# A MoE block on one core: skip terms moved from VectorE to ScalarE, and the router as four f32r passes one gate-up pair later

## The reference

```python
x = L0_attn_x
x = x + _L0_attn_ref(_layernorm(x, axis=-1), ...)      # Q (K^T V) scaled, times wo
x = x + _L0_ffn_ref(_layernorm(x, axis=-1), ...)
...
scores = jax.nn.sigmoid(x @ Wr)                        # 8 experts
_, idx = lax.top_k(scores + router_bias, TOP_K)        # two of them
w = jnp.take_along_axis(scores, idx, axis=-1)
w = w / (jnp.sum(w, axis=-1, keepdims=True) + 1e-09)
...
hid = jax.nn.silu(g) * u                               # experts 0 to 3, 256 -> 128 -> 256
mlp_out = jnp.einsum('tei,eih->teh', hid, Wd)
routed = jnp.einsum('te,teh->th', cw[:, :E_MLP], mlp_out)
routed = routed + cw[:, E_MLP:E_MLP + 1] * x
routed = routed + cw[:, E_MLP + 2:E_MLP + 3] * x
routed = routed + cw[:, E_MLP + 3:E_MLP + 4] * jax.nn.relu(x)
...
return routed + SHARED_SCALE * shared                  # shared: causal conv of 4 taps, per feature
```

## Time and profile before

| | us |
|---|---|
| median of 3 runs (lowest, highest) | 961.61 (958.10, 962.31) |
| the profiled execution: time | 958.19 |
| its span, first to last instruction | 956.4 |
| busy: TensorE, VectorE, GpSimd, ScalarE | 893.9, 832.3, 553.2, 544.4 |
| granted TensorE clock, mean share of full speed | 0.98 |

### The profile page before, as it was taken

How to read it: one execution, slowest core, us unless ns; L and a number is a source line. 1 busy time by engine, 2 the same in 40 slices (tenths; PEclk the granted TensorE clock), 3 DMA queues, 4 the chain that set the end, 5 groups by cost and what they waited for, 6 DMA issues and landing times.

```text
span 956.4 us, 16244 instructions
## 1 busy us (share of the span) xinstructions
PE 893.9 (93%) x5402; PEld 768.0 (80%) x5402; DVE 832.3 (87%) x2327; ACT 544.4 (57%) x1076; POOL 553.2 (58%) x491
## 2 busy tenths in 40 slices
PE   4578999999999999999999999999999999888887
PEld 3466888888888888888888888888888888777776
DVE  3677998999899998999999998999989987777885
ACT  3445566556656665666566556656655665444442
POOL 2145556667555566765556666555666764456653
PEclk9968999999999999999999999999999999999999
DMA  5302322223332221333322133332212222222111
GB/s 165 111 22 89 111 94 78 68 95 111 112 111 102 93 82 58 111 111 111 111 89 81 54 110 111 111 111 99 102 45 89 89 89 90 88 68 88 67 45 67
DMA packets 61011, 87.05 MB, mean 91 GB/s; under 512 B 4480, under 2 KB 56832, under 8 KB 56832
## 3 DMA queue, kind: packets, MB, share of 16 engines
q1 hardware_dynamic: 60928, 86.01, 25.9%
HBM read 68.96 MB, written 17.04 MB: 90 GB/s over the span
## 4 chain that ended last, share of the span: by engine, by line
DVE 43%; PE 20%; ACT 13%; POOL 11%; issue 11%; DMA 2%; POOLq 0%; ACTq 0%; SPq 0%; DVEq 0%
ACT x L719 5%; DVE hid L819 5%; ACT x L763 5%; DVE stats L865 4%; DVE acc L857 4%; POOL rstd L1073 4%; POOL enx L1108 3%; DVE acc L1019 3%; DVE idxf L902 3%; PE ps_gu L365 3%; PE ps_sh L464 3%; PE ps_gu L367 2%; PE ps_gu L366 2%; DVE acc L969 2%; PE ps_sh L474 2%
## 5 line engine op out<-in xcount | busy, mean ns | idle before, releaser
L1091 POOL TENSOR_TENSOR gate<-gate,cwb 128x512 f32<-128x512 f32 x128 | 169.3, 1323 | 148.2 <-ACT gate L647 99.8
L365 PE MATMUL ps_gu<-x2T_hi,wgu_hi 128*128 128x512 f32 x512 | 212.8, 416 | 0.9 <-DVE hid L819 0.8
L366 PE MATMUL ps_gu<-x2T_lo,wgu_hi 128*128 128x512 f32 x512 | 203.2, 397 | 0.0
L367 PE MATMUL ps_gu<-x2T_hi,wgu_lo 128*128 128x512 f32 x512 | 203.1, 397 | 0.0
L1108 POOL TENSOR_TENSOR enx<-inv_e,logits 128x32 f32<-128x32 f32 x32 | 178.0, 5561 | 6.7 <-ACT logits L640 6.5
L365 PE MATMUL ps_y<-wd_hi,hid_hi 128*128 128x256 f32 x512 | 156.6, 306 | 8.6 <-POOL hid_lo L1096 7.8
L367 PE MATMUL ps_y<-wd_hi,hid_lo 128*128 128x256 f32 x512 | 145.3, 284 | 0.0
L366 PE MATMUL ps_y<-wd_lo,hid_hi 128*128 128x256 f32 x512 | 145.2, 284 | 0.0
L836 DVE SCALAR_TENSOR_TENSOR conv<-x2T,conv_w,conv 128x512 f32<-128x512 f32 x192 | 143.0, 783 | 0.0
L1070 POOL TENSOR_TENSOR mv<-mv,eps_ln 128x4 f32<-128x4 f32 x64 | 12.8, 200 | 220.7 <-DVE mv L868 175.8
L647 ACT ACTIVATE gate<-ps_gu 128x512 f32<-128x512 f32 x128 | 75.9, 593 | 99.0 <-PE ps_gu L367 99.0
(11 more groups left out here) (100 smaller groups left out, 1834.9 us busy)
## 6 DMA issues: line engine op xcount, KB each, us to landing
cwb<-cw_rows SPq DMA_DIRECT2D x32, 1024.0 KB, 4.7
xa<-in_x SPq DMA_DIRECT2D x32, 512.0 KB, 6.7
acc<-in_x SPq DMA_DIRECT2D x32, 512.0 KB, 5.9
out<-acc SPq DMA_DIRECT2D x64, 256.0 KB, 2.2
cwb<-in_wg SPq DMA_DIRECT2D x4, 128.0 KB, 2.6
cwb<-in_wu SPq DMA_DIRECT2D x4, 128.0 KB, 2.6
cwb<-in_wd SPq DMA_DIRECT2D x1, 512.0 KB, 4.7
cw_rows<-cwT SPq DMA_DIRECT2D x32, 8.0 KB, 1.3
```

The lines of the kernel that those rows point to most:

```text
L365: nc.tensor.matmul(dst, a_hi, b_hi, start=start, stop=False, skip_group_check=True)
L366: nc.tensor.matmul(dst, a_hi, b_lo, start=False, stop=False, skip_group_check=True)
L367: return nc.tensor.matmul(dst, a_lo, b_hi, start=False, stop=stop, skip_group_check=True)
L1091: g.tensor_tensor(gate[:, e % 2], gate[:, e % 2], cwb[:, q, e], ALU.mult).then_inc(gatew_ready, 1)
```

## The change

Router: the weights `wr2` hold the high part of the router's 256 x 8 weights in columns 0 to 7, their low part in columns 8 to 15, and zeros. Four f32r matmuls of 512 columns (x2T high and low, two halves) give the logits of all 512 tokens transposed, ScalarE copies them (`logitsT`), TensorE transposes them back in four (`logits_transpose`), ScalarE copies 64 columns (`parts`), and GpSimd adds the two halves. On TensorE the router now stands behind gate_up 3, and the transposes behind gate_up 4. VectorE's `route` loses the `den` add to GpSimd and finds the chosen experts by `match_replace` instead of `max_index` and comparisons. The terms coef * x2 become acc * (1 + coef * rstd) + coef * shift on ScalarE, with the factors from four small GpSimd instructions (`skip_factors`). The relu add moves from behind hidden 1 to behind `q_low`.

```diff
             def router(st):
-                pe.wait_ge(x2T_ready, st.before("R", HC, HC))
+                if st.before("R") == 0:
+                    pe.wait_ge(wrlo_out, 1)
+                b, q = ps_sh[0], st.slot("R", 2)
                 pe.wait_ge(x2Tlo_ready, st.before("R", HC, 1))
-                b, q = ps_sh[0], st.slot("R", 2)
+                for c in range(HC):
+                    if c == 1:
+                        pe.wait_ge(x2Thi_ready, st.before("R", HC, HC))
+                    nc.tensor.matmul(b[:, :], wr2[:, c], x2T_hi[:, q, c], start=(c == 0), stop=False,
+                                     skip_group_check=True)
+                    if c == 1:
+                        pe.wait_ge(x2Tlo_ready, st.before("R", HC, HC))
+                    last = nc.tensor.matmul(b[:, :], wr2[:, c], x2T_lo[:, q, c], start=False, stop=(c == HC - 1),
+                                            skip_group_check=True)
+                last.then_inc(router_done, 1)
+
+            def logits_transpose(st):
+                pe.wait_ge(logitsT_ready, st.before("R", 1, 1))
                 for t in range(TG):
-                    for c in range(HC):
-                        last = nc.tensor.matmul(b[:, t * NE:(t + 1) * NE],
-                                                x2T[:, q, c, PAD + t * P:PAD + (t + 1) * P], wr_sb[:, c],
-                                                start=(c == 0), stop=(c == HC - 1))
-                last.then_inc(router_done, 1)
+                    last = nc.tensor.transpose(ps_sh[0][:, t * P:(t + 1) * P], logitsT[:, t * P:(t + 1) * P],
+                                               ident[:, :])
+                last.then_inc(parts_done, 1)
...
                 elif st.on("R"):
-                    pe.wait_ge(logits_ready, st.before("R", 1, 1))
+                    pe.wait_ge(parts_ready, st.before("R", 1, 1))
...
@@ -590,16 +616,17 @@
                     gate_up(st, 2)
                 if m_on:
                     chain_et(st)
-                if r_on:
-                    router(st)
+                if c_on:
+                    gate_up(st, 3)
                 if m_on:
                     pe.wait_ge(et_out, st.chains(2, 2))
-                if c_on:
-                    gate_up(st, 3)
-                if m_on:
                     chain_f(st)
+                if r_on:
+                    router(st)
                 if c_on:
                     gate_up(st, 4)
+                if r_on:
+                    logits_transpose(st)
                 if c_on:
                     conv_transpose(st)
...
-                if r_on:
-                    act.wait_ge(router_done, st.before("R", 1, 1))
-
-                    if st.later("R", 1):
-                        act.wait_ge(enx_ready, st.before("R"))
-                    copy(logits[:, :], ps_sh[0][:, 0:TG * NE]).then_inc(logits_ready, 1)
                 if m_on:
                     chain_copy(st, f_done, st.chains(1, 1),
                                [(f1[:, :], ps_gram[:, 0:H]), (f2[0:D, :], ps_gram[0:D, 0:H])], fhi_out)
                 if c_on:
                     hid_high(st, 0)
+                if r_on:
+                    act.wait_ge(router_done, st.before("R", 1, 1))
+                    copy(logitsT[:, :], ps_sh[0][:, :]).then_inc(logitsT_ready, 1)
                 if c_on:
                     silu(st, 2)
+                if r_on:
+                    act.wait_ge(parts_done, st.before("R", 1, 1))
+                    if st.later("R", 1):
+                        act.wait_ge(logits_ready, st.before("R"))
+                    copy(parts[:, :, :], ps_sh[0][:, :].rearrange("p (t n) -> p t n", t=TG)[:, :, 0:2 * NE])\
+                        .then_inc(parts_ready, 1)
+                if c_on:
 
                     q = st.slot("C", 2)
+                    act.wait_ge(skip_ready, st.before("C", 2, 2))
                     for t in range(TG):
-                        act.wait_ge(ident_added, st.before("C", TG, t + 1))
+                        a = acc[:, st.slot("C", 4), t]
+                        nc.scalar.activation(a, a, ACT.Identity, bias=skip_bias[:, q, t:t + 1],
+                                             scale=skip_scale[:, q, t:t + 1]).then_inc(ident_added, 1)
+                    for t in range(TG):
                         nc.scalar.activation(x2[:, q, t], x2[:, q, t], ACT.Relu, scale=cw[:, q, EM + 3, t:t + 1])\
                             .then_inc(relu_ready, 1)
                     hid_high(st, 1)
...
-                dve.wait_ge(enx_ready, st.before("R", 1, 1))
-                done(v.tensor_scalar(den[:, :], enx[:, :], 1.0, None, ALU.add))
-                after()
+                dve.wait_ge(den_ready, st.before("R", 1, 1))
                 done(v.reciprocal(flat(score[:, :, :]), den[:, :]))
                 after()
-                done(v.tensor_tensor(biased[:, :, :], score[:, :, :],
+                done(v.tensor_tensor(biased[:, :, 0:NE], score[:, :, :],
                                      bias8[:, :].unsqueeze(1).broadcast_to([P, TG, NE]), ALU.add))
                 turn(rt, st.before("R", RT, issued[0]))
                 for t in range(TG):
-                    done(v.max(top8[:, t], biased[:, t]))
+                    done(v.max(top8[:, t], biased[:, t, 0:NE]))
+                after()
+                done(v.tensor_copy(two8[:, :, 0:2], top8[:, :, 0:2]))
                 turn(rt, st.before("R", RT, issued[0]))
                 for t in range(TG):
-                    done(v.max_index(idx8[:, t], top8[:, t], biased[:, t]))
+                    done(v.match_replace(marked[:, t], two8[:, t], biased[:, t], TAKEN))
                 after()
-                done(v.tensor_copy(idxf[:, :, :], idx8[:, :, 0:2]))
-                after()
-                for n in range(2):
-                    done(v.tensor_tensor(hot[:, n], iota_f[:, :].unsqueeze(1).broadcast_to([P, TG, NE]),
-                                         idxf[:, :, n:n + 1].broadcast_to([P, TG, NE]), ALU.is_equal))
-                after()
-                done(v.tensor_tensor(chosen[:, :, :], hot[:, 0], hot[:, 1], ALU.add))
-                after()
-                done(v.tensor_tensor(raw[:, :, :], chosen[:, :, :], score[:, :, :], ALU.mult))
+                done(v.scalar_tensor_tensor(raw[:, :, :], marked[:, :, 0:NE], TAKEN, score[:, :, :],
+                                            ALU.is_equal, ALU.mult))
...
-                dve.wait_ge(cw_ready, st.before("R", 1, 1))
-                done(v.tensor_tensor(coef[:, q], cw[:, q, EM], cw[:, q, EM + 2], ALU.add))
...
@@ -1002,21 +1033,11 @@
                     hid_low(st, 0)
                     hidden(st, 1)
 
-                    q = st.slot("C", 2)
-                    dve.wait_ge(rt, st.before("C", RT, RT))
-                    for t in range(TG):
-                        a = acc[:, st.slot("C", 4), t]
-                        v.scalar_tensor_tensor(a, x2[:, q, t], coef[:, q, t:t + 1], a, ALU.mult, ALU.add)\
-                            .then_inc(ident_added, 1)
                 if m_on:
                     dve.wait_ge(fhi_out, st.chains(2, 2))
                     v.tensor_tensor(f2[D:P, :], ps_gram[D:P, 0:H], f1[D:P, :].bitcast(F32), ALU.subtract)\
                         .then_inc(flo_out, 1)
                 if c_on:
-
-                    dve.wait_ge(relu_ready, st.before("C", TG, TG))
-                    k = st.slot("C", 4)
-                    v.tensor_tensor(acc[:, k], acc[:, k], x2[:, st.slot("C", 2)], ALU.add).then_inc(relu_added, 1)
                     hidden(st, 2)
                 if r_on and c_on:
                     route(st)
@@ -1032,6 +1053,12 @@
                     hidden(st, 3)
                 if st.on("Q"):
                     q_low(st)
+                if c_on:
+
+                    dve.wait_ge(ident_added, st.before("C", TG, TG))
+                    dve.wait_ge(relu_ready, st.before("C", TG, TG))
+                    k = st.slot("C", 4)
+                    v.tensor_tensor(acc[:, k], acc[:, k], x2[:, st.slot("C", 2)], ALU.add).then_inc(relu_added, 1)
...
+            def skip_factors(st):
+
+                q = st.slot("R", 2)
+                pool.wait_ge(cw_ready, st.before("R", 1, 1))
+                if st.later("R", 2):
+                    pool.wait_ge(ident_added, st.before("R", TG, -TG))
+                g.tensor_tensor(coef[:, :], cw[:, q, EM], cw[:, q, EM + 2], ALU.add).then_inc(coef_ready, 1)
+                pool.wait_ge(coef_ready, st.before("R", 1, 1))
+                g.tensor_tensor(coef_rstd[:, :], coef[:, :], rstd2[:, q], ALU.mult).then_inc(coefr_ready, 1)
+                g.tensor_tensor(skip_bias[:, q], coef[:, :], shift2[:, q], ALU.mult).then_inc(skip_ready, 1)
+                pool.wait_ge(coefr_ready, st.before("R", 1, 1))
+                g.tensor_tensor(skip_scale[:, q], coef_rstd[:, :], ones4[:, :], ALU.add).then_inc(skip_ready, 1)
+
...
                 if r_on:
+                    pool.wait_ge(parts_ready, st.before("R", 1, 1))
```

(13 more changed lines are left out.)

77 lines of the change are left out of this document (51 added, 26 removed).

## The result

| | median us | lowest, highest | runs |
|---|---|---|---|
| before | 959.92 | 958.10, 962.31 | 4 |
| changed | 1074.72 | 1067.46, 1077.98 | 4 |

The changed kernel takes 1.119 times as long (95% interval 1.1154 to 1.1222). Its profiled execution took 1074.62 us, with a span of 1072.8 and a mean granted clock of 0.936. The forecast was 1055, range 1018 to 1095.

What follows compares the result with a forecast made beforehand. The prediction took a loop over TensorE, GpSimd's power and `hid_lo` 1 as the bound. Full steps 74, router steps 7 and 2, and clock 14 make 97 us on 958.2: 1055 us, range 1018 to 1095.

Steps and rivals of the forecast that it cites:

- The loop: TensorE, GpSimd's power and `hid_lo` 1 set the step, not VectorE; 27.05 us before, 29.90 after.
- old router's start (585.96) to the power: From where the router started before, behind gate_up 2, to the power on GpSimd: 5.66 us, where it was 2.16.
- stall before `down` 1: TensorE must stand for 3.1 us before every `down` 1, waiting for GpSimd's `hid_lo`.
- `hid_lo` 1 at 1.29: GpSimd's `hid_lo` 1 falls from 2.27 to 1.29 us, as the relu add on VectorE moves away.
- The first term, 15.92: TensorE from `down` 1 to the old router's start: 15.92 us, taken over unchanged from the old step.
- the 2.85 per step: Lengthening of the loop in each full step, from 27.05 to 29.90 us; 74 us over 26 steps.
- One step in three: Half clock behind the stall in 9 of the 26 steps, losing 1.65 us each: 14 us.
- The rival that named a low clock in nearly every step: Clock falls, or `hid_lo` 1 or relu add collides, in nearly every step: 1075 to 1120 us, chance 0.21.
- the first case: Main forecast: longer loop with the clock low in some steps, 1035 to 1075 us, chance 0.50.
- The tail: Five router steps after the full ones, each lengthened by half as much as a full step: 7 us.
- half of the second: The second is the rival "only the loop", clock staying at 1.00: 1005 to 1035 us, chance 0.20.
- the late relu add could collide: VectorE's moved add meets GpSimd's `hid_lo` 3 and pushes norm 2; lock up to 1.29 us, room about 1.

Runs made afterwards that it cites:

- the filled stall: Changed kernel plus twelve unused matmuls of 512 columns where TensorE stands before `down` 1: 1058.85 us; with the relu add moved as well, 1048.08 us.
- with the old router: Changed kernel with the eight-matmul fp32 router of before back behind gate_up 2, keeping the lighter VectorE step: 953.80 us.
- The fastest kernel: Lighter VectorE step with the fp32 router of before, relu add between hid_low 2 and residual, hid_low 1 on VectorE, hid_high 1 ahead of skip terms: 938.64 us.

## Why the prediction was right, and where its sizes were off

**The loop: right.** The step is held by TensorE, the power and `hid_lo` 1, and its terms came out as worked:

| term | predicted | in the step from 569.02 |
|---|---|---|
| gate_up 4's wait for hidden 0 | 0.50 | 588.77 less 588.29 = 0.48 |
| old router's start (585.96) to the power | 5.66 | 591.59 less 585.96 = 5.63 |
| power and `den` start to start, with its semaphore | 5.47 | 597.10 less 591.59 = 5.51 |
| `den` add | 0.25 | 597.31 less 597.10 = 0.21 |
| third gate product | 1.25 | 598.53 less 597.31 = 1.22 |
| `hid_lo` 1 | 1.29 | 1.27 |
| stall before `down` 1 | 3.1 | 2.92 |

Each step of it that was named as a sign is there: VectorE waits 7.37 for the third gate product and has (832.3 - 713.6) / 32 = 3.7 us less to do for each of the 32 groups, where about 4 were said. The kernel without the power shows the loop by its other side, 128 us less with the same work on TensorE.

**`hid_lo` 1 at 1.29: right.** It took 1.27 in place of the 2.27 of the earlier trace rows, with the relu add gone from beside it. By the port lock of the Trainium skill (page "SBUF — State Buffer", section "SBUF: two separate sides") it had to come back so, and the trace agrees.

**The first term, 15.92, fell short by 1.02.** From `down` 1 to the end of gate_up 2 it now took 585.96 - 569.02 = 16.94. The work is the same; 3.4 us of it ran at 0.50. What the loop takes at a full clock is seen in the kernel with the relu add moved. Its plain steps take 30.8 with a fall of the clock, and three without one took 29.74 to 29.79 from `down` 1 to `down` 1, where 29.90 was forecast. One of them:

```profile
287.31:317.06 29.75, 26.28 (x158) 22.50 (x158) 21.96 (x63) 18.97 (x38) 18.05 (x22) 1.00 0.26 90
```

So the 2.85 per step were right to about 0.1. In the changed kernel itself three steps without a fall took longer, 30.2 to 30.4, and in each of them the relu add stretched the power of norm 2 to 2.6. One of these:

```profile
411.55:441.99 30.44, 26.50 (x158) 22.53 (x158) 22.66 (x63) 18.89 (x38) 19.66 (x22) 1.00 0.27 87
```

From these steps, and from the filled stall, I read that low clock and long power delay the same joint, x2 and gate_up 2: the longer of the two counts, and they don't add up.

**The clock: mis-sized, and wrong in how often.** "One step in three" at 1.65, 14 us in all, was a choice from two rows. The clock fell in 22 of 26 steps, and a fall cost about 1.0 in a plain step and not 1.65; the rest did not lie on the loop. Taken out of the changed kernel as it stands, the low clock gives 16 us back, as the long power of norm 2 takes its place; with the add moved first it gives 22.8. That the term of 14 came near the first of these is luck, two errors against each other. 26 steps x (31.33 - 27.57) = 97.7, where the sum had 74 + 14 = 88. The rival that named a low clock in nearly every step was the true one in its frequency; at its price of 1.65 it gave 1084, and 1074.72 lies at the seam of it and the first case, 0.3 us inside the first.

**The tail: mis-sized.** The sum gave 7 us to the five router steps behind the full ones, "at half of it". The last four distances of two weights transposes are 123.8 us, against 106.6 before, so 17.2. They have the same stall before `down` 1 and, besides, one for x2 where TensorE has less to cover it:

```profile
1019.53 0.73 PE L478 MATMUL ps_sh<-ident,x 128*128 128x128 f32 x2 [1.70 <-ACT x L748]
```

The first router step was longer by 30.18 - 28.79 = 1.4, where 2 were said. The span's 1072.8 - 956.4 = 116.4 is 97.7 + 17.2 + 1.4, within 0.1. Of the 19 us by which the sum of 97 fell short, half thus lies in the full steps and half in the tail, and both fell short the same way. The range held the time by its width, and the 0.8 given to it was added up wrongly: first case, half of the second and half of the third are 0.50 + 0.10 + 0.105, about 0.7.

**The other signs.** The lighter `route` and the skip terms' room cost nothing, as said: both waited for the loop. That the late relu add could collide was among the rivals, with `hid_lo` 3 as its partner and "little is left" as its price. It does collide, but with the power of norm 2, and only where the two meet: in 3 of the 26 full steps of the changed kernel, in 17 with the old router, and in all 26 with gate_up 7 first, where it turns a gain of 24 us into a loss of 24. That partner was not seen.

**Where the lighter step's gain went.** VectorE's lighter work, alone, brings 7 to 8 us. The old loop doesn't pass through that work, as the prediction said. It also had 0.98 to come back at `hid_lo` 1, 25 us over the steps, and most of that was lost again. The `den` add on GpSimd takes 0.33 of it (5.72 from the power to the gate product, where it was 5.39). ScalarE does hid_high 1 behind the eight skip instructions, so `hid_lo` 1 waits 0.37 for it:

```profile
427.70 1.30 POOL L1109 TENSOR_TENSOR hid_lo<-hid,hid_hi 128x512 fp32r<-128x512 f32 x1 [0.37 <-ACT hid_hi L654]
```

And in the steps with a long norm power the step is 0.74 longer (27.08 against 26.35 in the same trace). The fastest kernel removes the last two.

## What to carry to other kernels

When two engines look full, write out the loop from one start of an instruction to its next before you shorten anything, and price a change by what it does to that loop alone: here a router with 0.4 us less TensorE work cost about 2.8 us per step before the clock, as its result reached the slow power two gate-ups later. A matmul form that needs one more input (here x2T's low part) is also bound to the engine that makes this input, and can't be moved freely. And a stall that a change opens in every step has a second price, the clock of the work behind it: filling it is worth a try, even with matmuls whose result nobody reads. Real work in their place gained no more here (1046.95 against 1048.08), and where it moved an add onto another engine's power it lost 24 us.
